# Last attention of a four-layer decoder: turned probabilities in a bank of their own, by quarters; queries and keys projected by channel for four batches

## The reference, cut to what matters

```python
qkv = x @ w_qkv + b_qkv                      # 256 -> 768
q, k, v = jnp.split(qkv, 3, axis=-1)         # 16 heads of 16 channels each
scores = jnp.einsum('bhql,bhkl->bhqk', q, k) / math.sqrt(16)
scores = jnp.where(q_ind < k_ind, -10000.0, scores)
probs = jax.nn.softmax(scores, axis=-1)
combined = jnp.einsum('bhqk,bhkl->bhql', probs, v)
x = _layernorm(x + combined @ w_out + b_out)
```

## Time and profile before

| | |
|---|---|
| median of 3 runs | 2803.95 us (2801.28 to 2804.85) |
| the profiled execution | 2791.89 us, of which the span is 2790.0 us |
| mean granted PE clock | 0.905 of full speed |
| busy over the span: PE, PEld, DVE, ACT, POOL | 80%, 61%, 67%, 47%, 13% |
| this sublayer, first DMA issue to last copy of x | 2329.67 to 2582.93 us |

### The profile page before, as it was taken

The page is one execution under the profiler, slowest core; times in us unless marked ns, Lnnn a source line. Parts: engine busy times, 40 slices in busy tenths (PEclk is TensorE's granted clock), DMA queues, the critical chain, the costliest instruction groups (busy, mean ns, idle before and its releaser), DMA issues. The chain is left out here.

```text
span 2790.0 us, 44753 instructions
## 1 busy us (share of the span) xinstructions
PE 2232.6 (80%) x18631; PEld 1707.2 (61%) x18631; DVE 1870.5 (67%) x3145; ACT 1324.7 (47%) x1693; POOL 349.6 (13%) x159
## 2 busy tenths in 40 slices
PE   7985368999999999998704979999997666886665
PEld 4654236777777777776602558999995434554443
DVE  5766757888778888778587243545545885776467
ACT  4652146666666666666343213333333364443237
POOL 0000112222222223222030600000000012000001
PEclk9997678999999999999856989999999888997878
DMA  3000021221221221221123541001000000000000
GB/s 138 2 1 13 9 75 52 52 56 55 76 58 50 59 57 47 66 69 34 41 94 102 121 176 42 13 28 45 19 30 8 1 1 25 1 1 1 16 1 31
DMA packets 159218, 123.09 MB, mean 44 GB/s; under 512 B 117440, under 2 KB 144832, under 8 KB 152512
## 3 DMA queue, kind: packets, MB, share of 16 engines
q1 hardware_dynamic: 155968, 116.25, 13.8%
q0 software_dynamic: 3072, 4.33, 0.9%
HBM read 102.88 MB, written 17.66 MB: 43 GB/s over the span
## 5 line engine op out<-in xcount | busy, mean ns | idle before, releaser
L1433 DVE SCALAR_TENSOR_TENSOR ctx_chan<-l1a_raw,l1a_cw,ctx_chan 128x1024 f32<-128x1024 f32 x192 | 230.8, 1278 | 19.4 <-ACT ctx_chan L1284 18.5
L1046 PE MATMUL banks<-x_chan,l1a_wp 128*128 128x512 f32 x512 | 230.2, 604 | 5.2 <-DMA l1a_wp<-in_l1a_wp_dram 5.2
L1010 POOL TENSOR_TENSOR l1a_sq<-ctx_chan 128x1024 f32<-128x1024 f32 x16 | 152.2, 9514 | 357.3 <-ACT ctx_chan L1288 357.3
L1046 PEld LDWEIGHTS banks<-x_chan,l1a_wp 128*128 128x128 f32 x512 | 97.9, 194 | 116.9 <-issue 110.7
L2535 PE MATMUL banks<-x_chan,l2a_wq 128*128 (+1 forms) x1024 | 124.5, 282 | 9.2 <-ACT l2a_ready L2400 4.9
L2535 PEld LDWEIGHTS banks<-x_chan,l2a_wq 128*128 128x128 f32 x1024 | 122.9, 199 | 11.2 <-issue 5.4
L1083 PE MATMUL banks<-l1a_wo,l1a_oT 128*128 128x256 f32 x512 | 121.7, 386 | 0.0
L1031 POOL TENSOR_TENSOR l1a_al<-l1a_aT,l1a_outer 128x1024 f32<-128x1024 f32 x32 | 74.8, 2357 | 319.2 <-DVE l1a_aT L1493 319.2
L2556 PE MATMUL banks<-l2a_wo,l2a_oT 128*128 128x256 f32 x512 | 113.2, 379 | 1.2 <-ACT l2a_oT L2424 1.2
L1054 PE MATMUL banks<-l1a_wz,x_chan 128*128 128x256 f32 x512 | 113.8, 380 | 0.0
L1054 PEld LDWEIGHTS banks<-l1a_wz,x_chan 128*128 128x128 f32 x512 | 97.7, 191 | 19.8 <-issue 7.2
(11 more groups left out here) (598 smaller groups left out, 5890.1 us busy)
## 6 DMA issues: line engine op xcount, KB each, us to landing
ctx_tok<-l1a_rows_mem SPq DMA_DIRECT2D x16, 1024.0 KB, 6.7
l1a_sq<-l1a_norm_mem SPq DMA_DIRECT2D x16, 1024.0 KB, 4.5
ctx_chan<-in_ctxT_dram SPq DMA_DIRECT2D x3, 2048.0 KB, 12.2
l1f_wgu<-in_l1f_wgu_dram SPq DMA_DIRECT2D x4, 1408.0 KB, 11.7
moe_sums<-l1x_zero SPq DMA_DIRECT2D x2, 2176.0 KB, 16.7
ctx_tok<-in_ctx_dram SPq DMA_DIRECT2D x2, 2048.0 KB, 11.5
l1a_wp<-in_l1a_wp_dram SPq DMA_DIRECT2D x8, 512.0 KB, 3.6
l1f_wgu<-moe_sums SPq DMA_DIRECT2D x8, 512.0 KB, 6.9
```

The costliest lines, as they stand in the source:

```text
L1010: P.tensor_tensor(sq[:, 0, :], conv[:, 0, :], conv[:, 0, :], ALU.mult).then_inc(s["k_squared"], 1)
L1046: mm = MM(ps[:, 2 * (u % 2) + q, :], wp[:, c, u * 128:(u + 1) * 128], g.xT[:, c, t0:t0 + 512], start=c == 0, stop=c == 1)
L1433: V.scalar_tensor_tensor(t, raw[:, u, :, j:j + S], cw[:, c, j:j + 1], t, ALU.mult, ALU.add).then_inc(s["conv_done" if step == 2 else "conv ...
```

## The change

`layer3_attention` gets a body of its own; the first layer keeps `narrow_attention`. Queries and keys are projected with the weights as the stationary operand, 128 channels by 512 tokens (four batches) at a time: four tiles (`project_qk(n)`, n modulo 4) serve four batches, and one tile of the next four batches is made in each of the first twelve iterations. ACT moves a tile and adds the bias there, the keys twice, once with the odd and once with the even heads multiplied by zero (`head_parity`), so that two heads share 32 rows and no packing is needed. The probabilities are turned by quarters of four heads into bank 4. Scores of batch i + 1 wait only for DVE's fill of batch i. Tiles after the fourth and the values share bank 5. The layer norm is done in two parts, 12 batches and 4. Host arrays `l3a_w`, `l3a_wo` and `l3a_bias` are permuted to the new order of heads. All of this is added, beside the old code for the first layer:

```diff
+def layer3_attention(nc, g):
+    HALF_HEADS = HEADS // 2
+    RING = 4
+    QUADS = B // GROUP
+    EARLY = 12
...
+        qT = [L.sb(f"qT{n}", [128, 2, GROUP * S]) for n in range(2)]
+        kT = [L.sb(f"kT{n}", [128, 2, 2, GROUP * S]) for n in range(2)]
...
+        def qk_bank(n):
+            return 4 + n % 2 if n < TILES else 5
...
+            sp.dma_start(w[:].rearrange("p c n -> p (c n)"), d["l3a_w"]).then_inc(s["w_loaded"], 16)
+            sp.dma_start(shifts[:], d["l3a_shifts"]).then_inc(s["shifts_loaded"], 16)
+            sp.dma_start(parity[:], d["head_parity"]).then_inc(s["shifts_loaded"], 16)
...
+            nc.gpsimd.tensor_tensor(k_shift[:], bc(shifts[:, 2:4], 2, 2), bc(parity[:], 1, 2), ALU.mult).then_inc(s["shifts_made"], 1)
+            nc.gpsimd.memset(vals[:], 1.0).then_inc(s["ones_made"], 1)
...
+            def qk_moved(n):
+                act.wait_ge(s["qk_proj"], n + 1)
+                now, m = n // TILES % 2, n % TILES // 2
+                if n % 2 == 0:
+                    A(qT[now][:, m, :], ps[:, qk_bank(n), :], ACT.Identity, bias=shifts[:, m:m + 1]).then_inc(s["qk_out"], 1)
+                else:
+                    for odd in range(2):
+                        ins = A(kT[now][:, m, odd, :], ps[:, qk_bank(n), :], ACT.Identity, bias=k_shift[:, m, odd:odd + 1],
+                                scale=parity[:, odd:odd + 1])
...
+            def probs_moved(i, n):
+                act.wait_ge(s["probs_turned"], 4 * i + n + 1)
+                A(probsT[:, 4 * n:4 * n + 4, :].rearrange("p q n -> p (q n)"), ps[:, 4, :], ACT.Copy).then_inc(s["probs_out"], 1)
...
+            for n in range(TILES):
+                qk_moved(n)
+            for i in range(B):
+                more = i + GROUP < B
+                if i:
+                    probs_moved(i - 1, 2)
+                if more:
+                    qk_moved(TILES + i)
+                if i:
+                    probs_moved(i - 1, 3)
+                if i > 1:
+                    output_moved(i - 2)
+                exps(i, 0)
+                if i:
+                    wide_moved(i - 1)
+                probs_moved(i, 0)
+                exps(i, 1)
+                probs_moved(i, 1)
...
+            for i in range(B):
+                if i:
+                    v.wait_ge(s["exped"], 2 * i)
+                for h in range(2):
+                    fill_future(i, h)
+                for h in range(2):
+                    shift(i, h)
+                if i:
+                    normalise(i - 1)
+                if 3 <= i + 2 < B:
+                    values_moved(i + 2)
+                if i > 1:
+                    add(i - 2)
+            moments(0, EARLY)
+            add(B - 2)
+            invert(0, EARLY, 1)
+            layer_norm(0, GROUP)
+            normalise(B - 1)
+            layer_norm(GROUP, EARLY)
+            add(B - 1)
+            moments(EARLY, B)
+            invert(EARLY, B, 2)
+            layer_norm(EARLY, B)
...
+            def project_qk(n):
+                q, m = n // TILES, n % TILES
+                if n >= 2:
+                    pe.wait_ge(s["qk_out"], n - 1 if n < TILES else n)
+                if n >= TILES:
+                    pe.wait_ge(s["v_out"], max(3, n - TILES + 2))
+                for c in range(DC):
+                    mm = mm_(ps[:, qk_bank(n), :], w[:, c, (m % 2 * 2 + m // 2) * 128:(m % 2 * 2 + m // 2 + 1) * 128], g.xT[:, c, q * 512:(q + 1) * 512], start=c == 0, stop=c == 1)
+                mm.then_inc(s["qk_proj"], 1)
...
+            def project_v(i):
+                if i:
+                    pe.wait_ge(s["v_out"], i)
+                if i >= 3:
+                    pe.wait_ge(s["qk_out"], min(TILES + i - 1, TILES * QUADS))
+                for c in range(DC):
+                    mm = mm_(ps[:, 7 if i < 3 else 5, 0:D], g.xT[:, c, i * S:(i + 1) * S], w[:, c, 2 * D:], start=c == 0, stop=c == 1)
...
+            def scores(i):
+                if i % GROUP == 0:
+                    pe.wait_ge(s["qk_out"], (i // GROUP + 1) * TILES)
+                if i:
+                    pe.wait_ge(s["filled"], 2 * i)
...
+                for q in range(4):
+                    for n in range(4):
+                        rows = slice(32 * n, 32 * n + 32)
+                        mm = mm_(ps[:, n, q * 128:(q + 1) * 128], qt[rows, q // 2, now], kt[rows, q // 2, q % 2, now], start=False, stop=q == 3)
+                mm.then_inc(s["scores"], 1)
...
+            def turn_probs(i, n):
+                pe.wait_ge(s["exped"], 2 * i + n // 2 + 1)
+                if i or n:
+                    pe.wait_ge(s["probs_out"], 4 * i + n)
+                else:
+                    pe.wait_ge(s["qk_out"], TILES)
+                for q in range(4):
+                    mm = turn(ps[:, 4, q * 128:(q + 1) * 128], probs[:, 4 * n + q, :], g.ident[:])
...
+            scores(0)
+            for i in range(B):
+                more = i + GROUP < B
+                if i:
+                    turn_probs(i - 1, 2)
+                if more:
+                    project_qk(TILES + i)
+                if i:
+                    turn_probs(i - 1, 3)
+                if i > 1:
+                    turn_output(i - 2)
+                if 3 <= i + 2 < B:
+                    project_v(i + 2)
+                if i:
+                    values(i - 1, 1)
+                if i > 1:
+                    output(i - 2)
+                turn_probs(i, 0)
+                if i:
+                    turn_back(i - 1)
+                if i + 1 < B:
+                    scores(i + 1)
+                turn_probs(i, 1)
+                values(i, 0)
+            turn_probs(B - 1, 2)
+            turn_output(B - 2)
+            turn_probs(B - 1, 3)
+            output(B - 2)
+            values(B - 1, 1)
+            turn_back(B - 1)
+            pe_turn_x(pe, g, s["ln_out"], s["x_turned"], s["x_turned_out"], stop=DC)
+            turn_output(B - 1)
+            output(B - 1)
+            pe_turn_x(pe, g, s["ln_out"], s["x_turned"], s["x_turned_out"], first=DC)
```

More of the change, by code:

```diff
@@ L163, in layer0_attention @@
     narrow_attention(nc, g, "l0a", rotary=True)
-def layer3_attention(nc, g):
-    narrow_attention(nc, g, "l3a", rotary=False)
 def narrow_attention(nc, g, name, rotary):
@@ L3298, in shape_constants @@
     c["l1f_consts"] = np.concatenate(places, 1).astype(np.float32)
+    c["head_parity"] = (q // HD % 2 == np.arange(2)[None, :]).astype(np.float32)
     c["window"] = np.where((k <= q) & ((k < 4) | (k >= q - 31)), 0.0, NEG).astype(np.float32)
@@ L3324, in layouts @@
     t["l0a_wo"] = by_partition(a["L0_attn_Wo"].T)
-    t["l3a_w"], t["l3a_wo"] = by_partition(a["L3_attn_w_qkv"]), by_partition(a["L3_attn_w_out"])
-    t["l3a_bias"] = np.concatenate([a["L3_attn_b_qkv"], a["L3_attn_b_out"]]).reshape(1, -1)
+    places = np.array([8 * (q // 2) + 2 * n + q % 2 for n in range(4) for q in range(4)])
+    w, b = a["L3_attn_w_qkv"], a["L3_attn_b_qkv"]
+    wv = w[:, 2 * D:].reshape(D, HEADS, HD)[:, places].reshape(D, D)
+    t["l3a_w"] = by_partition(np.concatenate([w[:, :2 * D], wv], 1))
+    t["l3a_wo"] = by_partition(a["L3_attn_w_out"].reshape(HEADS, HD, D)[places].reshape(D, D))
+    t["l3a_bias"] = np.concatenate([b[2 * D:].reshape(HEADS, HD)[places].reshape(-1), a["L3_attn_b_out"]]).reshape(1, -1)
+    t["l3a_shifts"] = np.concatenate([b[:D].reshape(2, 128).T, b[D:2 * D].reshape(2, 128).T], 1)
     t["mask"] = a["mask_BxS2_bk0"]
```

161 lines of the change are left out of this document (added).

## The result

| | before | after |
|---|---|---|
| median of the runs | 2803.8 us (4 runs) | 2753.45 us (4 runs: 2753.3, 2753.4, 2753.5, 2765.97) |
| ratio to before | | 0.983 (95% interval 0.981 to 0.985) |
| profiled execution | 2791.89 us, span 2790.0 | 2753.41 us, span 2751.5 |
| first DMA issue of the sublayer to its last copy of x | 253.3 us | 204.8 us |

What follows compares the result with a forecast made beforehand. A loop of waits, not one full engine, was taken to set the pace. Start -1.7, first to last fill -41.6 and end -5.5 sum to -48.8; taken from the median, 2755 us, with an 8-in-10 range of 2743 to 2769.

Steps and rivals of the forecast that it cites:

- start, to the first fill: Sublayer start: four projections and three of values without packing, first fill at 2349.1 instead of 2350.83, -1.7 us.
- first to last fill: Intervals between fills of the batches: 159.4 us instead of 201.0, -41.6 us.
- last fill to last copy of x: Sublayer end: twelve batches normalised while the last is on PE, 25.6 us instead of 31.1, -5.5 us.
- The old loop: Middle periods before: all of DVE's softmax, an exponential, a turn and the scores in series, 13.21 us; the change cuts it.
- PE's queue and two waits: Middle periods after: PE's work 9.4 plus waits for ACT's copies, 10.6 with queries, 11.5 with keys, mean 11.0.
- the stepping: PE's list walked through one iteration with start-to-start times of the old rows, giving 10.6 and 11.5 us.
- DVE is not the bound: Middle periods: exponential ready 1.3 us early; rival that DVE becomes the bound, 20 us less, 2735, chance 0.07.
- the 9.3 of the chain: Fill, fill, maximum, subtraction, exponential, first quarter, turn back, scores: sets 9.3 us in the three intervals without tiles.
- The clock was in the wrong place: Low PE clock expected late: 0.7 us added to each of the last three intervals, 1.0 to the end.
- The norm in two parts: Sublayer end: twelve batches normalised while the last is on PE, within the end's saving of 5.5 us.
- The rival of the slower sign: PE at half clock in the middle of the sublayer: period 18.5 us, about 2840, chance 0.03.
- The tile shape: PE changes tile shape six times a period instead of five: cost taken as 0, at most 0.1; 0.2 by the skill's rule.

Runs made afterwards that it cites:

- filler: Changed kernel with next scores behind the fourth quarter, plus 12 unread matmuls of 512 columns ahead of the first quarter: 2808.7 us, ratio 1.0026.
- the added transposes: Changed kernel plus eight overwritten transposes per batch ahead of the values of the second half: 2763.3 us (2 runs).
- The late kernel: Changed kernel with next scores behind the fourth quarter, here with 12 unread matmuls in PE's long wait: 2808.7 us, periods of 14.25.
- the third key copy: Changed kernel with each tile of keys copied by ACT once more, into a spare tile nobody reads: 2758.2 us (2 runs).
- The order that fills both: Changed kernel with query or key projection behind the second quarter, value projection ahead of the fourth, output ahead of values: 2741.9 us, ratio 0.9779.
- The filler gave 8.65: Changed kernel plus 16 unread matmuls ahead of the first quarter in the first iteration: 2751.3 us (2 runs), first interval 8.65 instead of 10.87.
- the experiment: Changed kernel with the layer norm in one part after the last batch, as before: 2757.7 us, last fill to last copy 30.4 us.
- the late scores: Changed kernel with next scores behind the fourth quarter again, without added matmuls: 2846.2 us, ratio 1.0165, periods of 17.0.

## Why the prediction was right

Its three terms against the rows:

| term | forecast | measured |
|---|---|---|
| start, to the first fill | -1.7 | -1.4 (19.7 us after the first DMA issue instead of 21.2) |
| first to last fill | -41.6 | -40.7 (160.4 instead of 201.0) |
| last fill to last copy of x | -5.5 | -6.4 (24.7 instead of 31.1) |
| sum | -48.8 | -48.5 |

- *The old loop is cut.* Shown: with the next scores put back behind all quarters, and the clock held up by filler, the periods are 14.25, longer than the 13.2 of before, although the packing is gone. So less PE work alone does not make the change fast; with the chain gone it counts, as the added transposes show. The late kernel is not the old loop restored: the projection and a third copy stand in its chain as well. That the packing cost nothing in the old order is read from PE's waits of 0.68 and 1.69 behind it; a kernel with the packing alone taken out was not run.
- *The period is PE's queue and two waits.* 10.6 and 11.5 were stepped, 10.67 and 11.43 came. The waits that I stepped count from the end of what a piece holds of the queue, those of the rows from the end of a row, which is later. In the stepping's terms the two came at 0.88 (2435.86 to 2437.20, less 0.46) and 1.12 (2440.43 to 2441.78, less 0.23), where I had 0.84 and 1.18. The pieces were off a little both ways: the key moves took 1.45 (0.775 each, the second starting 0.1 before the first ends) instead of 1.60 and the 128 x 512 projection held PE for 1.72 instead of 1.82, but transposes behind values hold it for 0.49 instead of 0.46, and the value projection for 1.04 instead of 0.95. My pieces of PE's work add up to 9.5 and not to the 9.4 that I wrote; 11.43 less the two waits is 9.43. That the second wait is on the path is shown by the third key copy, +0.67 in the periods with keys and nothing in the others. The order that fills both gives back 0.90 in the periods with queries, where the second was small, and 1.18 in those with keys.
- *DVE is not the bound.* Its wait for scores was 0.22, its slack of 2.24 ahead of `normalise`. The first exponential was ready at 2443.35, PE came to it at 2444.36: 1.0 us to spare where I had 1.3. With PE's queue shorter, the next limit shows: with the projection in the gap, the periods with queries came to 9.77 with PE waiting 0.19 for the exponential, near the 9.3 of the chain.
- *The clock was in the wrong place.* I had put 2.1 us of low clock into the last three intervals and 1.0 into the end. There it was not: PEclk is 1.00 in the windows of the last intervals and of the end, and the last intervals are 9.48, 9.47 and 9.14. It was in the first interval, which I had at 8.6 with nothing for the clock: PE waited 4.04 us for the first exponential and did mask and scores in 3.9 us instead of 2.1. The filler gave 8.65. The errors, +2.3 there, +0.5 in the ten middle periods, +0.3 in the start, -1.9 in the last intervals and -0.9 at the end, nearly cancel. That the sum is exact to 0.3 us is luck; with the errors of one sign alone it would have been off by 3.
- *The norm in two parts.* Up to 5.7 us of the 6.4 by the experiment, the clock that falls in one block of norms included. The forecast of 5.5 had 1.0 of low clock in it, which did not come.
- *The rival of the slower sign* was real as a mechanism: in the late scores the clock fell in the middle periods and cost 2.7 us each. In the changed kernel no wait in the middle is longer than 1 us, and PEclk was 1.00.
- *The tile shape.* The Trainium skill says in "TensorEngine Tiling (Array Packing)", Key Properties, that a change of mode drains the engine. From scores to the transposes of the second quarter, a change that before had no row, it is 1.10 us from start to start, as from scores to values before (1.11), which is a change as well. Four transposes behind values hold PE for 0.49, four behind work of the full shape 0.43 to 0.44. That is all that these rows show of it; the estimate of 0.2 more a period has hardly room, since PE's work of a period is 9.43 where the stepping's pieces, with nothing for it, add up to 9.5.

For the profiled execution the forecast was 2743.1, and it came at 2753.4: 10 us lie outside this sublayer, nearly all in the delta sublayer. The medians, which the forecast of 2755 is for, differ by 50.35. Why the delta sublayer takes anything from 1048 to 1058 us was not looked into.

## What to carry to other kernels

When no engine is full, write down the loop of waits and step each engine's list once with start-to-start times; a row's own duration is too long for what it holds of the queue. Taking one buffer out of the loop lets what stood in series run side by side; the next gain is then in what waits inside the fullest engine's own list, and order alone can fill it. Where PE has a long wait in every period, read its granted clock too: with one of 3.15 us the period lost 2.7 to the clock.

## What was not expected of the hardware

Useless matmuls made a kernel faster: twelve a batch took 2846.2 us to 2808.7. The granted clock was 0.80 over a period with one wait of 3.15 us and two shorter ones, and 1.00 with the long one filled to 0.56. In the changed kernel it was 1.00 in the middle, with waits of 0.69 and 0.97 in 11.4 us, and 0.69 in the first interval, with one of 4.04; before, it was 1.00 with waits of 0.68 and 1.69 in 13.2 us. Whether the longest wait counts or their sum, these runs do not separate.

The same wait of 4.04 us did not cost the same each time. In the changed kernel the first interval was 10.87; with the third key copy and with the added transposes, edits that leave PE's list up to the second fill as it is, it was 10.20 and 10.25. In the last of these the first quarter behind the wait was still at full length (0.66) and the scores were not (2.09 instead of 1.17).

Two activations in a row that read bias and scale from SBUF columns still overlap: 1.45 us for two of 0.775.
